# Filling the expert regions of a mixture-of-experts layer: eight fills in every body instead of sixteen near the end

## The reference

```
x = x + attn1(layernorm(x))          # Chebyshev feature attention, 16 heads of width 8, prefix sums over the sequence
y = layernorm(x)
y = y + attn2(layernorm(y)*g1 + b1)  # causal softmax attention, 16 heads of width 8
h = layernorm(y)*g2 + b2
logits = h @ gate_W + gate_b; top 2 of 8 experts, softmax over the two
moe = sum over the two experts of w_e * (gelu(h @ W1[e] + b1[e]) @ W2[e] + b2[e])
out = x + y + moe
```

## Time and profile before

| what | value |
|---|---|
| runs | 1501.98, 1501.0, 1501.69 us, median 1501.69 |
| the profiled execution, its own time | 1503.87 us |
| its span, first to last instruction | 1501.6 us |
| first half (dispatch ends) | up to 1184.8 us of the span |
| experts and sum | from there on |
| mean granted TensorE clock | 0.907 of 2.4 GHz |
| PE / DVE / ACT / POOL busy | 84% / 77% / 61% / 56% |
| moved by DMA | 116 MB, 77 GB/s over the span |

### The profile page before, as it was taken

One profiled execution on the slowest core, in us unless ns is written; L12 is line 12 of the kernel. 1 busy time (PEld: TensorE's weight loads), 2 busy tenths in 40 slices (PEclk: granted clock), 3 DMA queues, 4 the chain that ended last, 5 costly groups with the idle time before them and its releaser, 6 DMA issues.

```text
span 1501.6 us, 27731 instructions
## 1 busy us (share of the span) xinstructions
PE 1261.9 (84%) x8819; PEld 734.1 (49%) x8819; DVE 1152.0 (77%) x2622; ACT 912.0 (61%) x1795; POOL 847.7 (56%) x1077
## 2 busy tenths in 40 slices
PE   3466898999999999899998999988886399999970
PEld 1233254554545445454454544544343288888750
DVE  5658888888988888888988888856541588888765
ACT  1233376676756766567665766674564488888760
POOL 5776545667666676666767666532213246666570
PEclk8567799999999999999999999998998599999995
DMA  3032121422224222242321413223033212222238
GB/s 98 0 84 64 22 76 22 111 64 53 75 41 108 72 51 72 44 108 64 60 72 37 97 37 83 72 44 94 23 121 141 75 51 76 86 80 79 67 118 352
DMA packets 79344, 116.22 MB, mean 77 GB/s; under 512 B 15396, under 2 KB 61496, under 8 KB 74976
## 3 DMA queue, kind: packets, MB, share of 16 engines
q1 hardware_dynamic: 65888, 92.41, 23.7%
q0 software_dynamic: 9088, 17.33, 3.4%
q10 hardware_dynamic: 4224, 4.72, 0.9%
HBM read 58.29 MB, written 57.43 MB: 77 GB/s over the span
## 4 chain that ended last, share of the span: by engine, by line
PE 64%; DVE 15%; ACT 8%; issue 5%; DMA 3%; POOL 3%; another core or an unknown queue 1%; SPq 0%; POOLq 0%; DVEq 0%; ACTq 0%
PE back L1432 8%; PE scores L1412 8%; PE maxima L1373 8%; DVE nm L587 7%; PE front L1565 7%; PE back L1577 6%; PE front L1302 4%; PE maxima L1375 3%; DVE hn L461 3%; ACT pr L972 3%; PE front L1277 3%; PE scores L1415 2%; PE back L1252 2%; ACT rows L455 2%; DMA stack<-pairs 2%
## 5 line engine op out<-in xcount | busy, mean ns | idle before, releaser
L972 ACT ACTIVATE pr<-scores 128x384 f32<-128x384 f32 (+1 forms) x768 | 382.2, 525 | 232.0 <-PE scores L1415 199.0
L587 DVE TENSOR_REDUCE nm<-maxima 128x1 f32<-128x384 f32 (+3 forms) x704 | 426.7, 635 | 107.7 <-PE maxima L1375 95.5
L1412 PE MATMUL scores<-stack 98*128 98x512 bf16 (+3 forms) x1024 | 271.0, 314 | 32.7 <-ACT pr L972 29.8
L1373 PE MATMUL maxima<-stack 96*128 96x128 bf16 (+3 forms) x1024 | 258.0, 313 | 41.7 <-DVE nm L587 39.6
L1176 POOL DMA_INDIRECT xg<-rows,sloti x128 | 133.3, 1042 | 111.2 <-DVE sloti L657 71.4
L1412 PEld LDWEIGHTS scores<-stack 98*128 98x128 bf16 x1024 | 94.0, 102 | 197.6 <-ACT pr L972 123.7
L1415 PE MATMUL scores<-maskB,identb 128*128 128x128 bf16 (+1 forms) x768 | 189.0, 246 | 0.0
L1432 PE MATMUL back<-pr,vaug 128*9 128x512 f32 (+3 forms) x2048 | 182.5, 452 | 0.0
L1375 PE MATMUL maxima<-maskA,identb 128*128 128x128 bf16 (+2 forms) x704 | 177.4, 252 | 0.0
L1373 PEld LDWEIGHTS maxima<-stack 96*128 96x128 bf16 x1024 | 90.1, 100 | 170.1 <-DVE nm L587 81.3
L1241 POOL DMA_INDIRECT pairs<-xs x104 | 105.8, 1017 | 92.4 <-DVE xs L822 65.0
(11 more groups left out here) (222 smaller groups left out, 2542.5 us busy)
## 6 DMA issues: line engine op xcount, KB each, us to landing
stack<-spread SPq DMA_DIRECT2D x64, 384.0 KB
spread<-qs SPq DMA_DIRECT2D x96, 128.0 KB
spread<-ks SPq DMA_DIRECT2D x96, 128.0 KB
xs<-xg SPq DMA_DIRECT2D x39, 272.0 KB
stack<-pairs SPq DMA_DIRECT2D x8, 1024.0 KB
xg<-xs SPq DMA_DIRECT2D x17, 272.0 KB
xs<-in_x SPq DMA_DIRECT2D x16, 256.0 KB
acc<-xs SPq DMA_DIRECT2D x16, 256.0 KB, 2.3
```

Of the source, the lines that this page charges most:

```text
L587: v.tensor_reduce(nm[:, h:h + heads, t], ring(n)[:, 0:heads * (t + 1) * P].rearrange("p (h n) -> p h n", h=heads), AX.X, ALU.max, negate=T ...
L972: a.activation(pr[:, n % PR, 0:width], ringE[n % 2][:, 0:width], ACT.Exp).then_inc(W.exp_ready, 1)
L1373: k.matmul(ring(n)[:, at:at + (t + 1) * P], qst[p][0:MROW, h, t * P:(t + 1) * P], kst[p][0:MROW, h, 0:(t + 1) * P], start=(j == 0), stop=T ...
L1412: k.matmul(dst[:, at:at + T - t * P], kst[p][0:MROW + 2, h, t * P:(t + 1) * P], qst[p][0:MROW + 2, h, t * P:T], start=(t == tiles[0]), sto ...
```

## The change

Every body that has an f issues eight fills on SP, one per expert, of the rows f x 512 to f x 512 + 511 of its region, behind the stack loads. Before the dispatch of sequence t POOL waits for the fills up to f = t, in each of the eight calls. The sixteen fills from the counted rows on, the copy `tails` and the tile itself go, as does the wait of the last dispatch alone. The fills thus number 1 + 128 in place of 1 + 16.

```diff
@@ SP, body @@
-                if t == B - 2:
-                    sp.wait_ge(W.fill_ready, 2)
+                if f is not None:
                     for e in range(E):
-                        sp.wait_ge(W.tail_set, 16 * (2 * e + 1))
-                        at = sp.value_load(tails[0:1, e:e + 1], min_val=0, max_val=E * REGION - 2 * NB)
-                        for n in range(2):
-                            sp.dma_start(xg[bass.ds(at + n * NB, NB), :].rearrange("(p t) c -> p (t c)", t=QT), fill).then_inc(W.tail_set, 16)
+                        at = e * REGION + f * NB
+                        sp.dma_start(xg[at:at + NB, :].rearrange("(p t) c -> p (t c)", t=QT), fill).then_inc(W.tail_set, 16)
@@ DVE, slots @@
-                if b == B - 2:
-                    v.tensor_copy(tails[:, :], filled_to[:, :]).then_inc(W.fill_ready, 1)
@@ POOL, dispatch @@
-                if t == B - 1:
-                    wait_apart(pool, W.tail_set, 16 * (2 * E + 1))
+                wait_apart(pool, W.tail_set, 16 * (E * (t + 1) + 1))
```

More of the change, by code:

```diff
@@ L195, in block_kernel @@
         nblk = sb("nblk", [P, 3, E])
-        tails = sb("tails", [P, E], U32)
         spread = nc.dram_tensor("spread", (2, DH * len(TERMS6), H * T), BF16, kind="Internal").ap()
```

## The result

The change made the kernel slower by 2.8%: 1542.19 us median (1537.94 to 1549.34) against 1501.35 (1498.35 to 1501.98) of the kernel before beside it, four runs each, ratio 1.0281 [1.0239, 1.0322]. A ratio is taken over all runs of both kernels, so it can differ from the quotient of the two medians, by up to 0.2% in what follows; the brackets are its 95% interval. The profiled execution of the changed kernel took 1541.16 us with a span of 1539.0; before it was 1501.6, so 37.4 us of span are to be found.

A forecast was written before the change was run, and what follows sets the result against it. It took the kernel as bound by a chain of waits mostly through PE (busy 84%). Terms of 0 and one +1.6 us gave 1505.5 us profiled, 1503.3 against the median 1501.69; range 1496.4 to 1516 us.

The forecast's parts named there:

- held landings: Rival at POOL's wait before add_residual: dispatch lands later, (delay - 1.41) x 11, +8.7 us at 2.2 us; chance 0.27.
- DMA volume: DMA engines: 112 more fills take 84 us of DMA time, but nothing waits for bandwidth; cost 0.
- SP's issue: SP's queue behind the stack loads: issuing eight fills takes at most 4 us, with 34 us of cover; cost 0.
- the start: First two bodies: seventeen fills, 12.7 us of data, follow the first loads before SP's next work at 85.44; cost 0.
- POOL's waits: One more wait on POOL for each of 128 dispatches, on fills issued over 300 us earlier; cost 0.
- the removed work: DVE's copy, SP's eight register loads and eight waits, and the pairwise fills go; gain 0.
- The stalls from an unknown queue: Unexplained 5.13 us chain piece near the tail's fills: taken as 0, with up to 5.1 us gain kept in the range.
- the fast rival: Tail: the old fills caused the 5.13 us piece and static fills do not, so 1496.6 us; chance 0.20.
- the stall rival: Every body: fills beside dispatches cause stalls, 28 us less 5.1 at the tail, so 1525 us; chance 0.08.
- The slack of 1.41 us: Between the eighth dispatch's landing and ACT's rows: 0.75 us waiting for mvb plus 0.66 us at ACT are free.
- The fills against the eighth dispatch: Eleven bodies: dispatch lands 0.95 to 1.7 us late among the fills, costing 0.15 us each, +1.6 us (0 to 3.2).
- my own case: Whole kernel: 0 to +3.2 us, with POOL's wait before add_residual growing from 1.55 to 2.5 to 3.2 us; chance 0.45.

The follow-up runs named there:

- Runs 1: Changed kernel with its eight fills moved from behind the stack loads to behind the store of the residual: 1470.26 us, ratio 1.0009 to the kernel before.
- 9: Changed kernel with eight more fills per body and POOL's landing wait moved behind add_residual and the next norm: 1471.51 us, ratio 0.9997 to the kernel before.
- Run 8: Kernel before, with three memsets on POOL between landing wait and add_residual in eleven bodies: 1514.01 us, ratio 1.0289 to the kernel before.

## Why the prediction was wrong

The forecast was no change, 1503.3 us, with 1516.0 as the upper end; the kernel took 1542.19. The rival with the second largest chance, held landings, was the mechanism, but by its own price it would have come to 21 us at the delay that was measured, half of the loss.

*DMA volume, SP's issue, the start, POOL's waits, the removed work: right, each at nothing.* Runs 1 and 9 show it for volume and waits. In the body shown SP took 5.0 us for the eight fills, not the 4 that 0.50 each gave, and the spreads still came 36.6 us behind the x load. The start is not later. The train ended 12.7 us behind the last stack loads, as worked out.

*The stalls from an unknown queue: right to take neither rival.* The piece at 1173.35 stands where the sixteen fills had been, and there are none there now; it is 3.70 us in place of 5.13. It came some 36 us later than the 5.13 us, as everything there did. So the fills didn't make the piece, and the fast rival falls but for at most the 1.4 us between the two. No such piece lies in the eleven bodies, and the stall rival falls too.

*The slack of 1.41 us: about right.* 3.37 - 1.41 gives 1.96 where ACT waited 2.18; four fills (up to 1.59 us late) cost nothing and six do. Over the eleven bodies of the changed kernel POOL was 3.35 us behind 1.55 on average and ACT waited 2.30, so 1.05 us were free; in two of them `add_residual` took 1.6 to 1.7 us in place of 1.27, which used up some of it.

*The fills against the eighth dispatch: here it failed.* The step was: "The engines take turns between queues in the windows above (POOL's dispatches were issued and moved beside the loads), so I take one to two fills in front: 0.75 to 1.5 us, and its own 0.2 us at half the rate: 0.95 to 1.7 us late." Measured: 2.7 to 3.9 us later than 1.55, mean 3.35. That the upper end was nearest, "served behind everything, at 741.0 plus 0.2 of its own, 3.2 us late", is plain from the body at 757.88; six of the eleven bodies were beyond it. The windows showed that both kinds of transfer had moved in the same microsecond. They did not show how long one dispatch took, because nobody waited for those, and the prediction named this weakness itself and then leant on the argument. With 3.35 us in the sum it would have been (3.35 - 1.41) x 11 = 21 us, slower by 1.4%. The Trainium skill's rule of one packet per turn ("DMA: Bandwidth & Descriptors", queues, rings and completion order) would have made the sum 0, as the prediction read it, with one turn for the whole dispatch. The runs speak against that reading: 2.7 to 3.9 us are the time of about four to five fills at 0.75 us each. Whether a dispatch takes several turns, which the rule would allow, no row here shows. The 2 us of HBM access at high load, which the same page of the Trainium skill gives in its section on latency and other measured facts, would have made the landing 1.8 us later. It doesn't describe the hold, which goes from 0.6 us with four fills in front to 3.1 with eight.

*The price of lateness beyond the slack: mis-sized too.* I counted one microsecond for one. ACT's waits summed to 25.3 us, near to 21, but the time lost was 37 to 41. The rest goes with work that runs slower behind the waits: PE's busy time in the eleven bodies up by 15 us, at a granted clock of 0.93 in place of 0.96. Run 8 shows the same clock and the same kind of loss from POOL's lateness alone. Even the upper end of the prediction's delay, 3.2 us in all eleven bodies, gave only 20 us by a price of one; at the measured 1.3 to 1.8 it gives 26 to 36. That is why the range, which stopped at +14, missed by so much. (Its lower end stands as 1496.4 where the terms give 1496.6; nothing hangs on it.)

*The signs.* "ACT waits for POOL at rows by more than 0.5 us per body (held landings)" is what came, 1.75 to 3.11 us in each. POOL's wait passed the 2.5 to 3.2 us that I had named for my own case.

## What to carry to other kernels

A transfer that nobody waits for is free only as long as nobody waits for its neighbours: before you put a train of bulk DMAs anywhere, list the awaited landings that are issued while it runs, and what stands in order behind each. Here the same fills cost nothing behind the store, nothing between the stack halves, nothing when the wait came a few instructions later, and 2.8% where they stood. When a bound is open between "takes turns" and "behind everything" and nothing has ever waited for it, put the forecast at the far end, and price lateness beyond the slack at more than its own length.

## What the runs showed of the hardware

- A dispatch (128 rows of 544 bytes by an indirect DMA from POOL's queue) issued into a full SP queue landed 2.7 to 3.9 us later than the usual 1.55, with eight fills of 272 KB. With sixteen it waited 5.1 to 6.5 us in all, while data flowed for another five microseconds. Reads of 1.56 MB gave waits of 3.1 to 4.5 us. The mean wait goes 1.81, 2.40, 3.83, 4.96, 5.57 us with none, four, six, eight and sixteen fills (the first two not on the chip of the others). Why it gets through at about 5 us wasn't settled.
- In the changed kernel SP issued eight static fills in 5.0 to 6.0 us in the eleven bodies, 0.62 to 0.75 each. In the bodies at 98.18 and 145.01 eight took 3.9 and 4.1 us, about the 0.50 each of one alone.
- With a wait of 2 to 3 us on PE's way in each body the mean granted clock over 700 us was 0.93 in place of 0.96, in the changed kernel and in the kernel before with the memsets. The latter had 0.900 over its span, the three others on its chip 0.916 to 0.925.
- The kernel before took 1469.4 us on two chips and 1500 to 1501 in the two other sets of runs, with the same code. In every profiled kernel of those two sets the chain has one or two pieces of 3.7 to 5.1 us from an unknown queue (in the changed kernel at 1173.35 and 1439.78), and in none of the eight profiled on the first two chips has it a piece of that kind. The pieces are there with fills and without; they don't make up 30 us by themselves, and their cause stayed open.
